# Layer 0 of a four-layer network: gate and up products split into rounded parts, ternary buffers doubled, memory laid out anew

## The chip, the cores and the metric

The kernel runs on one core of one Trainium2 chip. The metric is the device time in microseconds; the median of three runs of the kernel before is given below. A core has a matrix engine (TensorE), three engines for element-wise work (VectorE, ScalarE, GpSimd), an engine that starts transfers (SyncE), an on-chip memory of 128 partitions (SBUF) and eight banks for matrix results (PSUM). The engines run their own queues in order and wait for each other by semaphores.

## The reference, cut to what matters

The network has four layers. Each takes a layer norm of x and adds an attention branch and a feed-forward branch of it to x. The change lies in layer 0. Its attention is a linear attention with 16 heads of 16 features in chunks; its feed-forward branch has weights that a cubic spline gives from control points. Its text isn't in full here; what is computed is this:

```
xn = layernorm(x)                                   # 1024 tokens, 256 features
q, k, v = heads(xn @ wq.T), heads(xn @ wk.T), heads(xn @ wv.T)
q = (q @ fq1.T + b) * (q @ fq2.T + b) * 16 ** -0.5  # k the same with fk1, fk2
o = q @ (running sum of k.T @ v of earlier chunks) + causal(q @ k.T) @ v
o = o * rsqrt(mean(o * o) + eps) * norm_w
gate = spline_reconstruct(gate_cp, 1024, 256)       # up too; down is 256 x 1024
h = silu(xn @ gate.T) * (xn @ up.T)
x = x + o @ wo.T + h @ down.T
```

Layer 3 has weights in bf16 that are made ternary: with s the mean absolute value of a group of 64, each weight becomes -s, 0 or s, as w + (w_hat - w). This depends on the weights alone, and the kernel does it during layer 0.

## The kernel before, in words

x is held as 8 tiles of 128 tokens by 256 features, its transpose xT as two tiles (k = 0, 1) of 128 features by 1024 tokens, in two blocks (b) of 512. All float32 products of layer 0 are plain float32 matmuls; the profile shows two records for each.

**Ahead of the loop.** TensorE transposes the norm of block 0, multiplies by wq and wk (`wide`, four products to raw0), makes the first spline block (`spline`, a product with all first cubics and one with all second cubics, each for gate, up and down), does the same for block 1, then the values in four products (`tall`, g_v0) with spline blocks 2 and 3 between. ScalarE copies xT (L1147), raw0 (L1172), the first cubics (`first_cubics`, L1154) and the values (`keep_v0`, L1165) out of PSUM, and casts the six parts of the ternary weights to bf16 (`cast_ternary`, L1160). VectorE puts the second cubics over the first where a mask says so (`second_cubics`, L1530) and sums the groups of the cast parts. The splines of gate, up and down then lie in V[0], V[1] and V[2]: 2048 columns each, in four blocks (s) of 512. Then `features` makes q and k in eight steps: TensorE gives two products of a step, ScalarE copies the one to f2s (L1190, L1192; two buffers), VectorE multiplies it with the other (L1567) and multiplies k by parity (L1559).

**The loop over eight chunks** c of 128 tokens. For each, TensorE runs in this order, written out by hand: scores of 16 heads to four banks (`scores0`, L661); gate and up of block 0 for the 128 hidden rows c (`gate_up0(c, 0, 0)` and `(c, 0, 1)`); keys by values (L699); gate of block 1; the queries by the running sum (L707) and the masked scores by the values (`values0`, L679); up of block 1. The eight banks are given in turn, ten to a chunk, so that the gate of block 1 gets the bank of the chunk's first score tile, and up of block 1 that of the second. VectorE runs: four causal masks (L1596); silu times up of block 0 (`hidden0`, L1590); the mask of keys by values (L1603) and the running sum (L1606); `hidden0` of block 1; and in the first six chunks two comparisons that give the signs of one ternary part (L1611, L1612). ScalarE does the silus (L1211) and keeps the outputs.

GpSimd copies the values of chunk c+2 by parity (`by_parity`, L2063) and turns the signs into a ternary part in four operations (L2071 to L2074), in the one pair of buffers tern_t; VectorE's signs of chunk c wait for the ternary part c-1.

After the loop come the group sums (L714), the down product and the output product. Layer 1 follows; its q and k products (`split_product`, L586 to L588) already use three products of rounded parts: hi*hi, hi*lo and lo*hi, with float32r operands.

In the page of the profile "arena" and "zone" are the two halves of the working memory.

Of the kernel before, what the change touches and what calls it, by code (L numbers as in the profile page):

```python
# [9 lines left out]
F32 = mybir.dt.float32  # L10
F32R = mybir.dt.float32r
# [7 lines left out]
P = 128  # L19
# [49 lines left out]
EPS3 = 2.0 ** -23  # L69
ARENA0 = 39400  # L70
ARENA, ZONE = 22500, 17930
ARENA1 = 28120
ALL = slice(None)

# [18 lines left out]
def build(nc, dram, out):  # L93

    ctx = ExitStack()
    with ctx:  # L96
# [3 lines left out]
        def sem(name):  # L100
            return ctx.enter_context(nc.semaphore(name))
# [17 lines left out]
        bw = lB[:, B_LW:B_LW + KD * D].rearrange("p (o i) -> p o i", o=KD)  # L119
        with nc.sbuf_tensor("arena0", [P, ARENA0], F32) as arena0:  # L120
            pass
        with nc.sbuf_tensor("arena1", [P, ARENA1], F32) as arena1:
# [56 lines left out]
        def step(ins, done):  # L179
# [38 lines left out]
            sem("hsq_ready"), sem("hsq_used"), sem("ms3_ready"), sem("std3_ready"), sem("rst_loaded"))  # L218
        held, x_rest, lA_rest = sem("held"), sem("x_rest"), sem("lA_rest")
        osq_summed = sem("osq_summed")  # L220
        qk_full, v_full, wv_hi, wv_split = sem("qk_full"), sem("v_full"), sem("wv_hi"), sem("wv_split")
# [21 lines left out]

        m = Carve(arena0)
        lA = m.cols(A_END + A_END % 2)
        hid0_at = m.at
        win, phase = m.cols(SPB), m.cols(SPB)
        hid0 = Carve(arena0, hid0_at).grid(NI, T)
        m.at = hid0_at + NI * T
        f2s_at = m.at  # L250
        basis = m.cols(2 * P)
# [3 lines left out]
        silu0 = Carve(arena0, f2s_at).grid(2, BW)  # L255
        V = [m.cols(SPB) for _ in range(3)]
        raw0_at = m.at
        raw0 = m.grid(4, T)
        oT0 = Carve(arena0, raw0_at).grid(NT, D)
        q0 = m.grid(KD, T)  # L260
        k0_at = m.at
# [4 lines left out]
        kpar = [m.grid(KD, T) for _ in range(2)]  # L266
        ktok, v0 = m.grid(NT, D), m.grid(NT, D)
        xn0_at = m.at
        kvbd = m.grid(NT, D)
        xn0 = Carve(arena0, xn0_at).grid(NT, D)  # L270
        kvtmp = m.cols(D)
        vflat = [m.cols(2 * VP) for _ in range(2)]
        vpar = [v[:, 0:2 * D].rearrange("p (r w) -> p r w", r=2) for v in vflat]
        tern_t = [m.cols(512).bitcast(BF16) for _ in range(2)]

# [264 lines left out]
        def _(pe):  # L540
# [125 lines left out]
            def gate_up0(c, b, n):  # L666
                wide(g_gu0[c][b][n], lambda k: V[n][:, k * I0 + c * P:k * I0 + (c + 1) * P], xT, b)

# [46 lines left out]
            pe.wait_ge(*g_gu0[NT - 1][NB - 1][1].ready)  # L715
            for p in range(NT // 2):
                tall(g_down0[p], p, lambda t: [(hid0[:, q, tok(t)], V[2][:, q * D:(q + 1) * D]) for q in range(NI)])
# [420 lines left out]
        def _(act):  # L1138
# [18 lines left out]
            def cast_ternary(n):  # L1157
                if n == 0:
                    act.wait_ge(raw_loaded, 16)
                act.activation(w16[:, n * I0:(n + 1) * I0], raw3[:, n * I0:(n + 1) * I0], ACT.Copy).then_inc(w16_cast, 1)  # L1160

            def keep_v0(p):
                g = g_v0[p]
                act.wait_ge(*g.full)
                act.activation(v0[:, 2 * p:2 * p + 2, :], g.ps.rearrange("p (t d) -> p t d", t=2), ACT.Copy).then_inc(g.ready_sem, 1)  # L1165

            for b in range(NB):
                keep_xT(0, [b])
                for mm in range(4):
# [311 lines left out]
        def _(dve):  # L1481
# [91 lines left out]

            dve.wait_ge(*g_ktok[-1].ready)
            dve.memset(kvbd[:, 0, :], 0.0).then_inc(kvbd_ready, 1)

# [15 lines left out]
            for c in range(NT):  # L1592
# [15 lines left out]
                if c < 6:  # L1608
                    if c:
                        dve.wait_ge(tern_ready, c)  # L1610
                    dve.tensor_tensor(by_group(tern_t[0]), tern_part(c), tern_group(2, c), ALU.is_gt)  # L1611
                    dve.tensor_tensor(by_group(tern_t[1]), tern_part(c), tern_group(3, c), ALU.is_lt).then_inc(tern_signs, 1)  # L1612
# [428 lines left out]
        def _(pool):  # L2041
# [16 lines left out]
            def by_parity(c):  # L2058
# [4 lines left out]
                pool.tensor_copy(own, v0[:, c, :].rearrange("p (g r e) -> p r g e", r=2, e=DK0)).then_inc(vpar_ready, 1)  # L2063

            by_parity(0)
            by_parity(1)
            for n in range(6):
                by_parity(n + 2)
                w, (t0, t1) = tern_part(n), [by_group(t) for t in tern_t]
                pool.wait_ge(tern_signs, n + 1)  # L2070
# [5 lines left out]


            def rest(pair, whole):
                return pool.tensor_tensor(pair[1].bitcast(F32R), whole, pair[0], ALU.subtract)  # L2079

# [217 lines left out]
```

## Time and profile before

| | |
|---|---|
| median of 3 runs | 724.84 us (724.24 to 725.26) |
| the profiled execution's own time | 729.03 us |
| its span, first to last instruction | 727.4 us |
| TensorE busy | 664.4 us, 91% of the span |
| VectorE busy | 521.8 us, 72% |
| ScalarE busy | 347.3 us, 48% |
| GpSimd busy | 320.5 us, 44% |
| mean granted TensorE clock | 0.98 |

PE is TensorE, DVE is VectorE, ACT is ScalarE and POOL is GpSimd. A profile is of one execution. Times in its views count from the span's start. "Idle before" is the time in which an engine had nothing to do ahead of an instruction, with what ended it. Records of consecutive matmuls overlap, so the distance from one start to the next tells what one costs, not its length.

### The profile page before, as it was taken

The page shows a single profiled execution, that of the slowest core. Times are in us where ns is not written, and L with a number is a line of the kernel's source. Part 1 is how long each engine was busy: PE and PEld are TensorE (multiplying, and loading weights), DVE is VectorE, ACT ScalarE, POOL GpSimd, SP SyncE. Part 2 cuts the span into 40 slices and gives each one's busy share as a digit, 9 for nine tenths or more (in the row PEclk, how much of TensorE's full clock was granted, in tenths as well). Part 3 has the DMA queues.
Part 4 walks back from the last instruction along what each step waited for, and adds up shares of the span by engine and source line. Part 5 has one row for each costly group of instructions (what it writes and reads, how often), then busy time and mean ns, then how long its engine had stood idle before and what let it go on. Part 6 is the DMA issues. An engine that isn't in the chain of part 4 may idle for free. (4 is left out here: it accounts for less than half of the span.)

```text
span 727.4 us, 13380 instructions
## 1 busy us (share of the span) xinstructions
PE 664.4 (91%) x4792; PEld 495.3 (68%) x4792; DVE 521.8 (72%) x1068; ACT 347.3 (48%) x749; POOL 320.5 (44%) x255
## 2 busy tenths in 40 slices
PE   3999999999799999999999999979988699877997
PEld 2445555588477988878787978869777447545666
DVE  4287686493599799797979986565366864579794
ACT  1575111300555565756555555744454542397732
POOL 1000988300457576674747478795185301300100
PEclk9999999999999999999999999999998889999999
DMA  8701000000601010010101011114212000100001
GB/s 261 300 2 59 1 2 1 1 1 0 223 17 38 23 34 24 7 36 20 34 18 36 22 38 34 35 32 142 66 52 66 1 0 1 36 1 0 2 1 58
DMA packets 14645, 31.34 MB, mean 43 GB/s; under 512 B 1837, under 2 KB 8587, under 8 KB 14029
## 3 DMA queue, kind: packets, MB, share of 16 engines
q1 hardware_dynamic: 12813, 26.46, 11.1%
q0 software_dynamic: 1536, 3.15, 1.5%
q10 hardware_dynamic: 256, 1.18, 0.6%
q8 instruction: 27, 0.44, 0.3%
q14 instruction: 13, 0.11, 0.1%
HBM read 26.59 MB, written 5.24 MB: 44 GB/s over the span
## 5 line engine op out<-in xcount | busy, mean ns | idle before, releaser
L586 PE MATMUL bank<-zone 128*128 128x256 f32 (+1 forms) x408 | 139.6, 342 | 18.2 <-DVE arena L1663 9.1
L588 PE MATMUL bank<-zone 128*128 128x256 f32 (+1 forms) x408 | 131.4, 322 | 0.0
L587 PE MATMUL bank<-zone 128*128 128x256 f32 (+1 forms) x408 | 131.2, 322 | 0.0
L2085 POOL TENSOR_TENSOR arena<-arena 128x512 f32<-128x512 f32 x64 | 82.3, 1287 | 64.1 <-ACT arena L1262 64.1
L586 PEld LDWEIGHTS bank<-zone 128*128 128x128 f32 x408 | 77.0, 189 | 39.3 <-DVE arena L1663 14.8
L2090 POOL TENSOR_TENSOR arena<-arena 128x512 f32<-128x512 f32 x64 | 83.3, 1301 | 27.7 <-DVE arena L1663 19.0
L588 PEld LDWEIGHTS bank<-zone 128*128 128x128 f32 x408 | 76.9, 188 | 6.2
L1281 ACT ACTIVATE arena<-arena 128x256 f32<-128x256 f32 (+1 forms) x128 | 62.0, 487 | 38.4 <-DVE arena L1672 32.6
L567 PE MATMUL bank<-xT,arena 128*128 128x512 f32 x160 | 78.0, 627 | 2.1 <-DMA arena<-in_lA 0.8
L587 PEld LDWEIGHTS bank<-zone 128*128 128x128 f32 x408 | 77.1, 189 | 3.5
L1672 DVE CUSTOM_DVE_ANT_0 arena<-bank,const 128x256 f32<-128x256 f32 (+1 forms) x128 | 45.6, 403 | 29.0 <-PE bank L773 22.1
L1688 DVE SCALAR_TENSOR_TENSOR x<-bank,arena,x 128x256 f32<-128x256 f32 x128 | 52.9, 470 | 13.3 <-PE bank L588 11.8
L1662 DVE TENSOR_TENSOR arena<-bank,arena 64x512 f32<-64x512 f32 x64 | 44.3, 693 | 18.2 <-ACT arena L1262 15.7
L803 PE MATMUL bank<-arena 128*128 128x128 f32 x256 | 50.8, 281 | 2.3 <-issue 2.3
L567 PEld LDWEIGHTS bank<-xT,arena 128*128 128x128 f32 x160 | 29.5, 197 | 34.1 <-issue 29.8
L1262 ACT ACTIVATE arena<-bank 128x512 f32<-128x512 f32 x64 | 37.5, 587 | 30.1 <-PE bank L588 30.1
L2079 POOL TENSOR_TENSOR zone<-arena,zone 128x512 fp32r<-128x512 f32 (+1 forms) x42 | 44.6, 1070 | 15.2 <-DMA arena<-in_cossin 6.1
L2048 POOL TENSOR_TENSOR lnw<-lnw,minus_half 128x4 f32<-128x4 f32 x8 | 8.2, 1020 | 97.6 <-DVE lnw L1500 97.6
L1023 PE MATMUL bank<-zone 128*128 128x512 f32 x128 | 36.8, 417 | 11.4 <-DVE arena L1918 9.2
L802 PE MATMUL bank<-arena 128*128 128x128 f32 x224 | 45.9, 288 | 0.0
L1663 DVE TENSOR_TENSOR arena<-bank,arena 64x512 f32<-64x512 f32 x64 | 43.7, 683 | 0.8
L803 PEld LDWEIGHTS bank<-arena 128*128 128x128 f32 x256 | 41.2, 197 | 3.9 <-issue 2.6
(289 smaller groups left out, 1345.9 us busy)
## 6 DMA issues: line engine op xcount, KB each, us to landing
arena<-in_qk SPq DMA_DIRECT2D x16, 256.0 KB
arena<-in_tern SPq DMA_DIRECT2D x1, 3072.0 KB, 22.6
arena<-in_wv SPq DMA_DIRECT2D x8, 256.0 KB, 2.9
arena<-in_wo SPq DMA_DIRECT2D x16, 128.0 KB, 2.1
arena<-in_wr SPq DMA_DIRECT2D x1, 1792.0 KB, 11.5
lB<-in_lB SPq DMA_DIRECT2D x1, 1288.5 KB, 25.1
x<-in_x SPq DMA_DIRECT2D x2, 512.0 KB, 8.0
xg_rows<-arena SPq DMA_DIRECT2D x1, 1024.0 KB
```

The source lines that it names most:

```text
L567: last = pe.matmul(g.ps, weight(k), act[:, k, b * BW:(b + 1) * BW], start=(k == 0), stop=(k == KD - 1))
L586: pe.matmul(dst, lhi, rhi, start=(n == 0), stop=False)
L587: pe.matmul(dst, lhi, rlo, start=False, stop=False)
L588: last = pe.matmul(dst, llo, rhi, start=False, stop=(n == len(terms) - 1 and not open_end))
L802: pe.matmul(ps[6 + g // 2][:, tok(t % TPB)], v1[:, t - 1, mine], pT1[:, t, 0, :], start=True, stop=False)
L803: last = pe.matmul(ps[6 + g // 2][:, tok(t % TPB)], v1[:, t, mine], pT1[:, t, 1, :], start=(t == 0), stop=True)
L1281: last = act.activation(S1[:, t, lo:], S1[:, t, lo:], ACT.Exp, scale=-1.0, bias=nmax[:, t:t + 1], accum_out=rsum[:, t:t + 1])
L1672: last = dve.tensor_tensor_reduce(S1[:, t, lo:], ps[2 + g % 2][:, tt * 2 * P + lo:(tt + 1) * 2 * P], winmask[:, lo:], -SC1, 3.0e38, ALU.ad ...
L1688: last = dve.scalar_tensor_tensor(out=x[:, t, :], in0=ps[bank][:, tt * D:(tt + 1) * D], scalar=rinv[:, t:t + 1], in1=x[:, t, :], op0=ALU.m ...
L2079: return pool.tensor_tensor(pair[1].bitcast(F32R), whole, pair[0], ALU.subtract)
L2085: pool.tensor_tensor(qraw[:, j, :], qraw[:, j, :], cosT[:, at], ALU.mult).then_inc(cos_done, 1)
L2090: pool.tensor_tensor((kT1, qT1)[j % 2][:, at], qraw[:, j, :], qsin[:, j, :], ALU.add).then_inc(qk_ready, 1)
```

## The change

- gate_up0 no longer multiplies V by xT in float32. xT and the splines of gate and up are each split into a rounded part (float32r) and the remainder, and each product becomes `split_product`: six matmuls of 512 columns.
- ScalarE makes the rounded parts: of xT in `round_x0(b)` (two operations a block, after the first cubics of the block), of the splines in `round_gu0(s)` (two a spline block, placed as the diff shows, s = 3 after the third of the eight feature steps). round_gu0 waits until all four remainders of xT are made.
- GpSimd makes the remainders: `rest_of_x0`, `rest_of_gu0`, one operation for each of ScalarE's.
- The parts of the spline weights (gu0p) lie where hid0, the hidden tiles, go: the remainder part of chunk c in the second half of its own hidden tile, the rounded part in the first half of the next chunk's tile.
- The two buffers of tern_t become two pairs; the signs of chunk c wait for ternary part c-2.
- The running sum kvbd lies over V[1], tern_t over V[0]; so VectorE waits for all remainders (gu0_split 8) before it clears kvbd, and for all ternary parts after the loop.
- basis, smask, V and lA and what follows are at other columns; a tensor "early" takes the first 7424 columns - 1280 of basis and mask and 6144 of V.

```diff
-ARENA0 = 39400
+ARENA0 = 40430
+EARLY = 2 * P + 3 * SPB + SPB // 2
...
+        kvbd = Carve(arena0, V_at + SPB).grid(NT, D)
...
+        x0p = [Carve(zone, at).grid(KD, T) for at in (m.at - ARENA, m.at - ARENA + KD * T)]
...
+        gu0p = [by_chunk(hid0_at - ARENA + T), by_chunk(hid0_at - ARENA + BW)]
+
+        def spline_block(n, s):
+            at = V_at + n * SPB + s * BW
+            return early[:, at:at + BW].rearrange("p (c i) -> p c i", c=TPB)
+
+        def split_block(part, n, s):
+            at = n * D + s // 2 * P
+            return gu0p[part][:, s % 2 * TPB:s % 2 * TPB + TPB, at:at + P]
...
             def gate_up0(c, b, n):
-                wide(g_gu0[c][b][n], lambda k: V[n][:, k * I0 + c * P:k * I0 + (c + 1) * P], xT, b)
+                g = g_gu0[c][b][n]
+                reuse(g)
+                split_product(g.ps, [(cut(parts(gu0p), ALL, c, slice(n * D + k * P, n * D + (k + 1) * P)),
+                                      cut(parts(x0p), ALL, k, slice(b * BW, (b + 1) * BW))) for k in range(KD)]).then_inc(g.full_sem, 1)
...
                 if c == 0:
-                    pe.wait_ge(*g_spl[-1][-1][1].ready)
+                    pe.wait_ge(x0_split, NB * KD)
+                if c % TPB == 0:
+                    pe.wait_ge(gu0_split, 6 + c // TPB * 2)
...
+            def round_x0(b):
+                act.wait_ge(xT_ready, KD * (b + 1))
+                for k in range(KD):
+                    act.activation(x0p[0][:, k, b * BW:(b + 1) * BW].bitcast(F32R), xT[:, k, b * BW:(b + 1) * BW], ACT.Copy).then_inc(x0_hi, 1)
+
+            def round_gu0(s):
+                act.wait_ge(x0_split, NB * KD)
+                for n in range(2):
+                    act.wait_ge(*g_spl[s][n][1].ready)
+                    act.activation(split_block(0, n, s).bitcast(F32R), spline_block(n, s), ACT.Copy).then_inc(gu0_hi, 1)
...
                 first_cubics(b)
+                round_x0(b)
             for b in range(NB):
                 keep_v0(2 * b)
+                if b == 0:
+                    round_gu0(0)
                 cast_ternary(2 + 2 * b)
                 keep_v0(2 * b + 1)
                 cast_ternary(3 + 2 * b)
                 first_cubics(NB + b)
+                round_gu0(1 + b)
...
+                if n == 2:
+                    round_gu0(3)
...
+            dve.wait_ge(gu0_split, 8)
             dve.memset(kvbd[:, 0, :], 0.0).then_inc(kvbd_ready, 1)
...
-                    if c:
-                        dve.wait_ge(tern_ready, c)
+                    if c >= 2:
+                        dve.wait_ge(tern_ready, c - 1)
...
+            dve.wait_ge(tern_ready, 6)
...
+            for b in range(NB):
+                rest_of_x0(b)
+            pool.wait_ge(x0_split, NB * KD)
+            rest_of_gu0(0)
             by_parity(0)
             by_parity(1)
+            for s in range(1, 4):
+                rest_of_gu0(s)
```

## Rows read from the trace of the kernel before

**Rows 1.** Busy time and instructions of each engine, granted clock and transfers, the loop.

```profile
60.00:145.00 85.00, 84.47 (x680) 45.73 (x675) 55.52 (x86) 20.25 (x39) 54.95 (x30) 1.00 0.04 14
```

**Rows 2.** Order of time, TensorE: start, length, instruction; loop's start, one chunk, loop's end.

```profile
59.03 1.17 PE L661 MATMUL bank<-arena 32*128 32x128 f32 x32 [0.89 <-DVE arena L1559]
...
79.13 1.17 PE L661 MATMUL bank<-arena 32*128 32x128 f32 x32
80.23 3.70 PE L567 MATMUL bank<-xT,arena 128*128 128x512 f32 x8
83.77 0.61 PE L699 MATMUL bank<-arena 128*128 128x128 f32 x4
84.22 1.88 PE L567 MATMUL bank<-xT,arena 128*128 128x512 f32 x4
85.94 0.61 PE L707 MATMUL bank<-arena 128*128 128x128 f32 x4
...
87.49 1.98 PE L567 MATMUL bank<-xT,arena 128*128 128x512 f32 x4
89.40 1.17 PE L661 MATMUL bank<-arena 32*128 32x128 f32 x32
...
141.56 3.60 PE L714 MATMUL bank<-arena,const 128*128 128x512 f32 x8
```

**Rows 3.** Order of time, VectorE, in the same chunk and the next.

```profile
80.15 1.23 DVE L1611 TENSOR_TENSOR arena<-w,tern_s 128x1024 bf16<-128x1024 bf16 x1 [0.22 <-POOL w L2074]
81.29 1.42 DVE L1612 TENSOR_TENSOR arena<-w,tern_s 128x1024 bf16<-128x1024 bf16 x1
82.64 2.47 DVE L1596 TENSOR_TENSOR arena<-bank,const 128x512 f32<-128x512 f32 x4
...
86.07 1.11 DVE L1606 TENSOR_TENSOR arena<-arena 128x256 f32<-128x256 f32 x1
89.51 0.69 DVE L1590 TENSOR_TENSOR arena<-bank,arena 128x512 f32<-128x512 f32 x1 [2.33 <-PE bank L567]
90.94 1.23 DVE L1611 TENSOR_TENSOR arena<-w,tern_s 128x1024 bf16<-128x1024 bf16 x1 [0.73 <-POOL w L2074]
```

**Rows 4.** Order of time, GpSimd, in the same chunk.

```profile
80.18 1.46 POOL L2063 COPY arena<-arena 128x256 f32<-128x256 f32 x1
82.80 2.13 POOL L2071 TENSOR_TENSOR arena<-arena 128x1024 bf16<-128x1024 bf16 x1 [1.16 <-DVE arena L1612]
85.00 1.89 POOL L2072 TENSOR_TENSOR arena<-arena,tern_s 128x1024 bf16<-128x1024 bf16 x1
```

**Rows 5.** Order of time, TensorE: first and last of layer 1's first twelve split matmuls.

```profile
193.07 0.47 PE L586 MATMUL bank<-zone 128*128 128x512 f32 x1 [1.62 <-POOL zone L2079]
...
195.71 0.40 PE L588 MATMUL bank<-zone 128*128 128x512 f32 x1
```

**Rows 6.** Order of time, GpSimd and VectorE, in layer 2.

```profile
577.92 4.51 POOL L2165 TENSOR_TENSOR x<-x,bias 128x2048 f32<-128x2048 f32 x1 [1.50 <-DVE arena L1503]
...
578.48 3.98 DVE L1857 TENSOR_SCALAR arena<-arena 128x2 f32<-128x2 f32 x1
```

**Rows 7.** Order of time, TensorE, ahead of the loop.

```profile
27.08 7.13 PE L567 MATMUL bank<-xT,arena 128*128 128x512 f32 x16 [0.75 <-ACT xT L1147]
```

**Rows 8.** Groups by line and form: busy, mean ns of one, idle before; rounding and remainder.

```profile
L1428 ACT ACTIVATE zone<-arena 128x512 fp32r<-128x512 f32 x16 | 9.9, 616 | 0.0
...
L2079 POOL TENSOR_TENSOR zone<-arena,zone 128x512 fp32r<-128x512 f32 x25 | 32.0, 1292 | 11.5 <-DMA arena<-in_cossin 6.1 <-ACT zone L1346 5.4
```

**Rows 9.** Busy time of ScalarE alone, first cubics of block 1 to the features.

```profile
35.69:50.17 14.48, 10.66 (x18) 1.00 0.01 2
```

**Rows 10.** Busy time of TensorE, then the granted clock, in three stretches.

```profile
475.00:478.00 3.00, 1.22 (x11) 1.00 0.00 0
550.00:553.00 3.00, 0.71 (x13) 0.81 0.44 109
553.00:556.00 3.00, 3.00 (x15) 0.50 0.08 27
```

More of the change, by code:

```diff
@@ L120, in build @@
         with nc.sbuf_tensor("arena0", [P, ARENA0], F32) as arena0:
+            pass
+        with nc.sbuf_tensor("early", [P, EARLY], F32) as early:
             pass
@@ L219, in build @@
         held, x_rest, lA_rest = sem("held"), sem("x_rest"), sem("lA_rest")
+        x0_hi, x0_split, gu0_hi, gu0_split = sem("x0_hi"), sem("x0_split"), sem("gu0_hi"), sem("gu0_split")
         osq_summed = sem("osq_summed")
@@ L241, in build @@
         y_rows = nc.dram_tensor("y_rows", (SLOTS + 1, D), F32, kind="Internal").ap()
[L244 to L249, printed above, removed]
+        m = Carve(early)
         f2s_at = m.at
-        basis = m.cols(2 * P)
+        basis = Carve(arena0, m.at).cols(2 * P)
+        m.at += 2 * P
         smask4 = m.cols(SPB // 2).bitcast(I32)
@@ L255, in build @@
         silu0 = Carve(arena0, f2s_at).grid(2, BW)
+        kvtmp = Carve(arena0, f2s_at + 2 * BW).cols(D)
+        V_at = m.at
         V = [m.cols(SPB) for _ in range(3)]
+        tern_t = Carve(arena0, V_at).cols(SPB).bitcast(BF16).rearrange("p (s n e) -> p s n e", s=2, n=2)
+        kvbd = Carve(arena0, V_at + SPB).grid(NT, D)
+        assert m.at == EARLY
+        m = Carve(arena0, m.at)
+        lA = m.cols(A_END + -A_END % 16)
         raw0_at = m.at
@@ L259, in build @@
         oT0 = Carve(arena0, raw0_at).grid(NT, D)
+        win, phase = [Carve(arena0, m.at + n * SPB).cols(SPB) for n in range(2)]
         q0 = m.grid(KD, T)
@@ L266, in build, with by_chunk @@
         kpar = [m.grid(KD, T) for _ in range(2)]
[L267 to L271, printed above, removed]
+        ktok = m.grid(NT, D)
+        hid0_at = m.at
+        assert hid0_at >= ARENA
+        hid0 = m.grid(NI, T)
+        m.cols(BW)
+        x0p = [Carve(zone, at).grid(KD, T) for at in (m.at - ARENA, m.at - ARENA + KD * T)]
+        m.cols(2 * KD * T + 128)
         vflat = [m.cols(2 * VP) for _ in range(2)]
         vpar = [v[:, 0:2 * D].rearrange("p (r w) -> p r w", r=2) for v in vflat]
-        tern_t = [m.cols(512).bitcast(BF16) for _ in range(2)]
+        xn0 = Carve(arena0, m.at).grid(NT, D)
+        v0 = m.grid(NT, D)
+        def by_chunk(at):
+            return zone[:, at:at + NI * T].rearrange("p (c w) -> p c w", c=NI)[:, :, 0:BW]
+        gu0p = [by_chunk(hid0_at - ARENA + T), by_chunk(hid0_at - ARENA + BW)]
[5 more added lines that the diff above has]
+            return gu0p[part][:, s % 2 * TPB:s % 2 * TPB + TPB, at:at + P]
         def by_group(t):
@@ L715, in _ @@
             pe.wait_ge(*g_gu0[NT - 1][NB - 1][1].ready)
+            pe.wait_ge(*g_spl[-1][-1][1].ready)
             for p in range(NT // 2):
@@ L1608, in _ @@
                 if c < 6:
-                    if c:
-                        dve.wait_ge(tern_ready, c)
-                    dve.tensor_tensor(by_group(tern_t[0]), tern_part(c), tern_group(2, c), ALU.is_gt)
-                    dve.tensor_tensor(by_group(tern_t[1]), tern_part(c), tern_group(3, c), ALU.is_lt).then_inc(tern_signs, 1)
+                    if c >= 2:
+                        dve.wait_ge(tern_ready, c - 1)
+                    dve.tensor_tensor(by_group(tern_t[:, c % 2, 0, :]), tern_part(c), tern_group(2, c), ALU.is_gt)
+                    dve.tensor_tensor(by_group(tern_t[:, c % 2, 1, :]), tern_part(c), tern_group(3, c), ALU.is_lt).then_inc(tern_signs, 1)
             dve.wait_ge(ln3_ready, 1)
+            dve.wait_ge(tern_ready, 6)
             after(k2)
@@ L2063, in by_parity, with rest, rest_of_x0, rest_of_gu0 @@
                 pool.tensor_copy(own, v0[:, c, :].rearrange("p (g r e) -> p r g e", r=2, e=DK0)).then_inc(vpar_ready, 1)
+            def rest(pair, whole):
+                return pool.tensor_tensor(pair[1].bitcast(F32R), whole, pair[0], ALU.subtract)
+            def rest_of_x0(b):
+                for k in range(KD):
+                    pool.wait_ge(x0_hi, KD * b + k + 1)
+                    rest([t[:, k, b * BW:(b + 1) * BW] for t in x0p], xT[:, k, b * BW:(b + 1) * BW]).then_inc(x0_split, 1)
+            def rest_of_gu0(s):
+                for n in range(2):
+                    pool.wait_ge(gu0_hi, 2 * s + n + 1)
+                    rest([split_block(part, n, s) for part in range(2)], spline_block(n, s)).then_inc(gu0_split, 1)
+            for b in range(NB):
+                rest_of_x0(b)
+            pool.wait_ge(x0_split, NB * KD)
+            rest_of_gu0(0)
             by_parity(0)
             by_parity(1)
+            for s in range(1, 4):
+                rest_of_gu0(s)
             for n in range(6):
                 by_parity(n + 2)
-                w, (t0, t1) = tern_part(n), [by_group(t) for t in tern_t]
+                w, (t0, t1) = tern_part(n), [by_group(tern_t[:, n % 2, i, :]) for i in range(2)]
                 pool.wait_ge(tern_signs, n + 1)
@@ L2075, in _ @@
                 pool.wait_ge(tern_ready, n + 1)
-            def rest(pair, whole):
-                return pool.tensor_tensor(pair[1].bitcast(F32R), whole, pair[0], ALU.subtract)
             def turn_qk(h, js, base=HEAD0):
```

## The prediction, made before the changed kernel was run

> **What bounds the kernel now.** I read the busy shares of the stretch of layer 0's eight chunks first, then TensorE's order of time in one chunk, then VectorE's and GpSimd's in the same chunk. TensorE is busy for 84.47 of 85 us there at full clock [rows 1], so a cheaper product is worth something only as long as no other engine takes its place. The loop runs from the scores at 59.03 to the group sums at 141.56, 82.5 us [rows 2]. A full chunk is 10.27 us (79.13 to 89.40): scores 1.10, two feed-forward products 3.54, keys by values 0.44, third product 1.72, read of the running sum and values 1.55, fourth product 1.91. Beside it runs the ternary ring: VectorE's two sign operations start at 80.15 and again at 90.94 [rows 3], 10.79 apart; in between lie the signs (to 82.71) and GpSimd's four operations on the only buffer pair (82.80 to 90.9) [rows 4]. It is the longer of the two and takes over within a few chunks, once its lead is used up: eight chunks at TensorE's pace would be 81.3.
>
> **Part 1, the products.** A plain product is two float32 matmuls, 1.71 to 1.91 us here. A split one is six single-pass matmuls. The row that shows them back to back is layer 1's: twelve from 193.07 to the start of the last at 195.71 [rows 5], so 0.23 each with 0.11 once for the change of kind. A pair of products then takes 2.87 (3.54 before), a single one 1.49 (1.72 and 1.91 before). TensorE's own chunk falls from 10.27 to 8.98 (0.67, 0.23 and 0.42 less). If nothing else held it: chunk 0 8.4 (no read of the sum), chunks 1 to 6 9.0, chunk 7 8.5: 70.9, a gain of 11.6 us. That is the upper end for this part.
>
> **Part 2, the doubled ternary buffers.** The ring through one buffer pair is broken: the signs of chunk c now wait for ternary c-2. But VectorE and GpSimd come to work at the same time on operands in SBUF, and the trace shows what that costs. A VectorE operation on 2 elements takes 3.98 us, started at 578.48 while GpSimd's addition on x ran from 577.92 to 582.43 [rows 6]: it waits for the whole of the other's instruction. The running sum (L1606) at 86.07 ends 0.29 after GpSimd's operation that started at 85.00 [rows 3, 4]. The other way, GpSimd's copy issued at 80.18 ends at 81.64, 0.35 after the first sign operation gives way at 81.29, and the second sign operation is lengthened to 1.42: GpSimd gets in between the two. Operations with one input in PSUM (the four masks, 2.47 in all at 82.64 [rows 3] with GpSimd busy) don't suffer.
>
> Before, the ring itself kept signs and ternary work apart; that cover is gone. GpSimd needs 8.1 us for a ternary part and 0.4 for the copy (0.35 of it behind the sign operation), so in a chunk of 9 to 10 us one of its operations nearly always runs when the signs are issued. Signs then: rest of the running operation about 0.8 (0 to 1.9), first sign 1.1, a whole GpSimd operation 1.8 (it waited, so it goes next) in most cases, second sign 1.1: 4.4, against 2.28 alone (80.15 to 81.29, twice); bounds 2.3 and 5.9. What is queued behind them on VectorE is the four masks of the next chunk, and TensorE waits for the first mask to free the bank of its third product. Counted from the end of a fourth product: hidden 0.7, signs 4.4, first mask 0.65, then third product 1.49, sum and values 1.55, fourth product 1.49: 10.3 to 10.4, more than TensorE's 8.98. The signs of chunk 0 meet an idle GpSimd, those of chunk 1 and 2 are at 3.8 to 4.1 (GpSimd has not yet filled its time), so the chunks are 8.4, 9.0, 9.8, 10.1, 10.4, 10.4, 10.4, 8.5: 77.1. The same count for the code before gives 82.4 against 82.5 read. **Loop: 5.4 us less**, between 11.6 less (no meeting) and 2.4 more (signs at 5.9 make the five chunks 11.8, 84.9 in all).
>
> The exclusive use is also a rule of the Trainium skill (SBUF — State Buffer, Who interferes with whom): a VectorE instruction with two SBUF inputs and a GpSimd instruction that reads SBUF shut each other out for the whole instruction. The trace agrees: 3.98 us for two elements. It speaks against doubling, whose overlap it takes back.
>
> The waits moved with it cost nothing: ternary 5 is done some 6 us before VectorE leaves the loop, and GpSimd's copies for chunk n+2 stand one ternary part behind, over 10 us before TensorE needs them.
>
> **Part 3, the rounding ahead of the loop.** ScalarE gets four rounded pieces of x and eight blocks of weights, each 128x512 from SBUF. Such a rounding is 0.62 long and a remainder on GpSimd, of which there are twelve, 1.29 [rows 8]. Back to back I count a rounding at 0.52: an estimate from the masks and the running sum, whose records overlap the next start by about 0.1. VectorE and ScalarE set this stretch, since the features need the last spline block.
> - The two roundings of x's first half stand in ScalarE's queue ahead of the copies of the second xT, for which TensorE already waits 0.75 at 27.08 [rows 7]: 1.05 late.
> - From the first cubics of block 1 to the features (14.48 us) ScalarE works 10.66 [rows 9]: 3.8 idle, of which the last 1.8 is the wait for VectorE's block 3. Into it go, ahead of the last cubics, six roundings (3.15) and a wait for GpSimd's last remainder of x (two remainders 2.6, less the copy that ScalarE does meanwhile and their overlap: 1.8). 4.95, of which 2.0 fit in the idle pieces: 2.9 late. The two of block 2 fit into the last 1.8.
> - The two of block 3 (1.05) stand in the features, where ScalarE and VectorE take turns: 0.9.
> Sum **4.8 us more**. Below: 3.0, if the wait for x's remainders is shorter and more of it falls in idle time; above: 6.1, if VectorE's predicated copies (mask in SBUF; the trace has none beside a GpSimd read) hold up one remainder, 1.29, on the way to ScalarE's first weights; 7 with a second. The last remainder of the weights ends near 60; VectorE's new wait for it stands behind all its feature products and parities, and TensorE's scores, which need most of these, start at 59.03 + 4.8: it is covered by some 4 us; without that it would cost up to the remainder's 1.29.
>
> **Part 4, the layout** only names other columns; the DMAs, their order and sizes stay: 0, within the 0.5 us to either side by which the runs shown differ.
>
> **The sum.** -5.4 + 4.8 = -0.6 us. The profiled execution took 729.03 with a span of 727.4 and would take 728.4; the median of the runs is 4.2 lower, 724.84, and becomes 724.2. Nothing behind the loop changes, and it is bound by TensorE again at once.
>
> **Rivals.**
> - A. The forecast: exclusive use eats half the product gain, the prologue the rest. 724.2, own range 722 to 727. Chance 0.42.
> - B. The meeting is milder: the sign pair stays together (GpSimd gets in only before or after), signs 2.6 to 3.3. Chunks near 9.1, with two of 9.7: loop 72.4, -10; or none at all, -11.6. With +4.8: 718.0 to 719.6. For it: in the ring before, only a short copy shows the order. Against it: 1.42 instead of 1.23 for the second sign in every chunk. 0.20.
> - C. Slower: TensorE's clock falls among the features. There it will wait about 1.7 us for the last first cubics and 1.2 for VectorE's part of block 3, with one feature group of some 0.8 us before, between and after. In the trace the granted clock was 0.81 of full speed in a stretch in which TensorE worked only 0.71 of 3 us, and 0.50, the 1.2 GHz level, in the next; it was 1.00, 2.4 GHz, in another with 1.22 of 3 [rows 10]. At 1.2 GHz the six feature groups after that take 1.64 instead of 0.82 and pass the 0.8 of ScalarE and VectorE: +2 to +3.2 over A, 726.2 to 727.4, say 727. It decides if the clock falls ahead of the fourth group. For it: the gaps; against: they come one by one, with groups between. 0.25.
> - D. The prologue costs 3 or less with A's loop: 722.4 or less. ScalarE's order is written out, so little speaks for more. 0.13.
>
> By the Trainium skill (TensorE: Matmul & The Clock Gate, the warm start-to-start rule of N / 2.4 + 2.5 ns) a 512-column matmul would follow each 216 ns; rows 5 show 230 to 240. By the rule TensorE's chunk would be 8.6, an estimate, and only chunks 0, 1 and 7 would show it, 1 us in all; the row decides.
>
> **How the numbers follow.** About 0.2% (1.45 us) can be told from no change. A splits into 0.12 faster, 0.24 same, 0.06 slower; B is faster; C 0.05 same, 0.20 slower; D 0.10 faster, 0.03 same: 0.42, 0.32, 0.26. The range takes in B's upper part and C with a dearer prologue: 718.6 to 728.6; the likeliest one's own is 722 to 727.
>
> **What the profile after would show.** The third product in a full chunk at 1.5; scores 8.4 and 9.0 apart in the first two chunks and 10 to 10.5 in chunks 3 to 6; the sign operations at 1.2 to 3 us each with GpSimd running through, and TensorE's third product waiting for the masks. Scores of chunk 0 near 63.8 instead of 59.03; a ScalarE gap of 1.8 in front of the first weight rounding, and features 4 us later. It is wrong if signs stay at 1.2 each (B), if the clock row of the features is below 1.00 (C), or if the scores start before 62 (D).

## The result, and the profile after

The changed kernel takes 727.65 us (median of 6 runs, 726.99 to 727.96), the kernel before 725.05 beside it (6 runs, 724.24 to 725.71): ratio 1.0033, 95% interval 1.0021 to 1.0044. It is slower, by 0.3%. The forecast was 724.2, inside a range of 718.6 to 728.6. The profiled execution took 727.57 us, with a span of 726.0.

TensorE's order of time in the trace of the changed kernel: start, length, instruction, and in brackets the idle time before. Split products are L611 to L613, scores L686, keys by values L729, the sum's read L737, values L707, group sums L744.

```profile
28.15 7.13 PE L592 MATMUL bank<-xT,arena 128*128 128x512 f32 x16 [1.77 <-ACT xT L1178]
...
64.03 1.17 PE L686 MATMUL bank<-arena 32*128 32x128 f32 x32 [0.65 <-DVE arena L1607]
...
85.50 0.61 PE L729 MATMUL bank<-arena 128*128 128x128 f32 x4
87.38 0.50 PE L611 MATMUL bank<-zone 128*128 128x512 f32 x1 [1.27 <-DVE arena L1645]
...
88.87 0.61 PE L737 MATMUL bank<-arena 128*128 128x128 f32 x4
89.41 1.08 PE L707 MATMUL bank<-arena 128*32 128x128 f32 x32
90.42 0.49 PE L611 MATMUL bank<-zone 128*128 128x512 f32 x1
...
92.01 1.17 PE L686 MATMUL bank<-arena 32*128 32x128 f32 x32
...
108.82 0.49 PE L611 MATMUL bank<-zone 128*128 128x512 f32 x1 [1.55 <-DVE arena L1645]
...
143.47 3.59 PE L744 MATMUL bank<-arena,const 128*128 128x512 f32 x8
```

Against [rows 2], the third product now takes 1.49 (87.38 to 88.87) where it took 1.72, and the values follow. But ahead of it stands a wait for VectorE's mask (L1645) that the chunk of [rows 2] did not have. The scores of the first chunk start at 64.03 instead of 59.03, the group sums at 143.47 instead of 141.56: a loop of 79.4 us instead of 82.5. The idle time at 28.15 is 1.77 where [rows 7] have 0.75.

VectorE and GpSimd in chunk 4 of the changed kernel (signs L1660 and L1661; ternary operations L2140 to L2143; copy by parity L2113), first VectorE, then GpSimd:

```profile
103.36 1.71 DVE L1660 TENSOR_TENSOR arena<-w,tern_s 128x1024 bf16<-128x1024 bf16 x1
105.00 3.16 DVE L1661 TENSOR_TENSOR arena<-w,tern_s 128x1024 bf16<-128x1024 bf16 x1
108.08 2.47 DVE L1645 TENSOR_TENSOR arena<-bank,const 128x512 f32<-128x512 f32 x4
```

```profile
97.59 2.15 POOL L2140 TENSOR_TENSOR arena<-arena 128x1024 bf16<-128x1024 bf16 x1
99.82 1.90 POOL L2141 TENSOR_TENSOR arena<-arena,tern_s 128x1024 bf16<-128x1024 bf16 x1
101.80 2.19 POOL L2142 TENSOR_TENSOR arena<-arena,w 128x1024 bf16<-128x1024 bf16 x1
104.07 3.01 POOL L2143 TENSOR_TENSOR w<-w,arena 128x1024 bf16<-128x1024 bf16 x1
107.14 1.27 POOL L2113 COPY arena<-arena 128x256 f32<-128x256 f32 x1
108.38 2.14 POOL L2140 TENSOR_TENSOR arena<-arena 128x1024 bf16<-128x1024 bf16 x1
```

The reader is to see three things. The two engines alternate: the first sign is issued at 103.36 and gets its turn as the third operation ends (101.80 + 2.19 = 103.99), GpSimd's fourth operation is issued at 104.07 and is lengthened to 3.01, and the second sign takes 3.16 because it waits for the end of that fourth operation at 107.08 (104.07 + 3.01). GpSimd has no idle time in brackets any more: its cycle, 97.59 to 108.38, is 10.79 us, and that is what a chunk lasts, as long as VectorE's sign cycle was before (80.15 to 90.94 [rows 3]). And the third operation takes 2.19 us. I had carried over 8.1 us for the four from [rows 4]; the rows of before for the third and fourth, which had no contention at all, are these:

```profile
97.77 1.95 POOL L2073 TENSOR_TENSOR arena<-arena,w 128x1024 bf16<-128x1024 bf16 x1
99.80 1.89 POOL L2074 TENSOR_TENSOR w<-w,arena 128x1024 bf16<-128x1024 bf16 x1
```

The same operation of the same shape on the same data has become 0.24 us longer without anything beside it; the experiments below find out why.

### The profile page after: what moved, and what is told of

The parts are those of the page before. It is cut to its first block and busy times, and to the rows that moved or that the text cites. A ratio compares the mean times of both kernels' runs of the same rounds, so it can differ in the third digit from the quotient of the medians.

```text
span 726.0 us, 13538 instructions
## 1 busy us (share of the span) xinstructions
PE 653.4 (90%) x4856; PEld 506.2 (70%) x4856; DVE 533.8 (74%) x1068; ACT 353.0 (49%) x761; POOL 340.7 (47%) x267
## 5 line engine op out<-in xcount | busy, mean ns | idle before, releaser
L611 PE MATMUL bank<-zone 128*128 128x256 f32 (+1 forms) x472 | 167.6, 355 | 22.4 <-DVE arena L1645 7.4
L613 PE MATMUL bank<-zone 128*128 128x256 f32 (+1 forms) x472 | 157.0, 333 | 0.0
L612 PE MATMUL bank<-zone 128*128 128x256 f32 (+1 forms) x472 | 156.9, 332 | 0.0
L611 PEld LDWEIGHTS bank<-zone 128*128 128x128 f32 x472 | 89.2, 189 | 49.0 <-DVE arena L1713 12.8
L613 PEld LDWEIGHTS bank<-zone 128*128 128x128 f32 x472 | 89.2, 189 | 9.1
L612 PEld LDWEIGHTS bank<-zone 128*128 128x128 f32 x472 | 89.4, 189 | 5.3
L1310 ACT ACTIVATE arena<-bank 128x512 f32<-128x512 f32 x64 | 37.6, 587 | 31.0 <-PE bank L613 30.9
L834 PE MATMUL bank<-arena 128*128 128x128 f32 x256 | 49.5, 275 | 2.3 <-issue 2.3
L833 PE MATMUL bank<-arena 128*128 128x128 f32 x224 | 44.9, 282 | 0.1
L2244 POOL TENSOR_TENSOR arena<-arena,minus_half 128x4 f32<-128x4 f32 x2 | 2.9, 1468 | 86.2 <-DVE arena L1982 86.2
L1291 ACT ACTIVATE arena<-bank 128x512 f32<-128x512 f32 x32 | 19.1, 598 | 47.6 <-PE bank L613 47.6
```

The lines of the kernel that those rows point to most:

```text
L611: pe.matmul(dst, lhi, rhi, start=(n == 0), stop=False)
L612: pe.matmul(dst, lhi, rlo, start=False, stop=False)
L613: last = pe.matmul(dst, llo, rhi, start=False, stop=(n == len(terms) - 1 and not open_end))
L833: pe.matmul(ps[6 + g // 2][:, tok(t % TPB)], v1[:, t - 1, mine], pT1[:, t, 0, :], start=True, stop=False)
L834: last = pe.matmul(ps[6 + g // 2][:, tok(t % TPB)], v1[:, t, mine], pT1[:, t, 1, :], start=(t == 0), stop=True)
```

## The experiments

All are compared with the kernel before, measured beside them. "Scores" is the time from TensorE's transposes of block 1 (25.28 in the changed kernel) to the first scores; "loop" is from there to the group sums. From the group sums to the issue of the transfer of layer 1's first weights all have 41.5 to 41.8 us. What lies behind that differs from one profile to the next: 539.6 to 543.1 us, but 534.8 to 536.8 in the four of e8 to e11, and 544.3 in the profile shown ahead of the prediction. So the profiled waypoints tell the terms apart, and the ratios check the sum. In the kernel before: scores 33.8, loop 82.5, GpSimd's third and fourth operation 1.96 and 1.89.

**e0, the kernel before again.**

> The kernel before, unchanged, for a second profile. Theory: the profiled execution shown before the prediction (729.0 us against a median of 724.8) was held up behind the loop, by a late transfer at 184 to 192 us and lower granted clock at 545 to 560 us; another one takes 725 to 726 us, with the loop again from 59.0 to 141.6 us. Rival: recording itself costs 4 us, and it is 729 again.

723.53 us, scores 33.8, loop 82.5. The waypoints repeat to 0.02. The span is 5.5 us shorter than that of the profile shown ahead of the prediction: 1.0 of it lies ahead of the transposes, 4.5 behind the loop.

**e1, the doubled buffers alone.** Edit, to the kernel before:

```diff
-        tern_t = [m.cols(512).bitcast(BF16) for _ in range(2)]
+        tern_t = m.cols(2 * I0).bitcast(BF16).rearrange("p (s n e) -> p s n e", s=2, n=2)
...
-                    if c:
-                        dve.wait_ge(tern_ready, c)
+                    if c >= 2:
+                        dve.wait_ge(tern_ready, c - 1)
```

> The kernel before with the doubled ternary buffers alone. Theory (port): VectorE's signs and GpSimd's operations exclude each other, so GpSimd's cycle stays 10.8 us (8.1 of its own, 0.4 copy, 2.3 of signs) with or without the second pair; loop 82 to 83 us, total 724.5 to 725.5 us. Rival (ring): the wait for the one pair was what held the chunks at 10.8, without it they run at TensorE's 10.27; loop 81.2 us, total 723.7 us or less.

723.9 us, 0.9992 (0.9975 to 1.0009); loop 81.6, third and fourth operation 1.96 and 1.89, GpSimd's cycle 10.61 instead of 10.79. The loop lies between the two expectations, 82 to 83 and 81.2, since most of its chunks run at TensorE's 10.27 here and only the seventh reaches 10.61. What tells is the cycle: doubling alone frees 0.2 us a chunk. The ring through one buffer pair was broken, and the alternation keeps nearly all of its length.

**e2, the changed kernel with one buffer pair.** Edit: `tern_t[:, 0, ...]` and `wait_ge(tern_ready, c)` in place of `c % 2` and `c - 1`.

> The changed kernel with one ternary pair and the old wait. Port: the cycle of 10.8 us is the same, only one early chunk can lose; 727.6 to 728.8 us. Ring: the loop falls back to the 82.5 us of the kernel before; 730.5 us or more.

729.41 us, 1.0072 (1.005 to 1.0094); scores 38.7, loop 81.8, the cycle 11.3 (two chunks in the middle, 12.85 and 9.71, have that as their mean). So doubling is worth 2.3 us in the loop beside the split products, and it did not cause the loss. One pair with these products should have given at most the 10.8 of before. It gave 11.3, and its third and fourth operations take 2.19 and 2.14.

**e3, all the rounding, but plain products.** Leaves out the products with remainder parts:

```diff
-                split_product(g.ps, [...]).then_inc(g.full_sem, 1)
+                wide(g, lambda k: gu0p[0][:, c, n * D + k * P:n * D + (k + 1) * P], x0p[0], b)
```

> The changed kernel with all roundings and remainders made, but gate and up as plain float32 products of the rounded parts, so that the remainders are not used (the output leaves out the two cross products). Theory: the start of the loop stays at 64.0 us, 5.0 later than before, and the loop is 82 to 83 us again: 729.5 to 731 us. The split products are then worth the 3 us between this and the changed kernel. Rival: the rounding is cheap and the loss lies in the loop; then this is at 725 to 727 us.

732.63 us, 1.0123 (1.0093 to 1.0152); scores 38.7, loop 83.9. Beside e1, with the same products and the same doubled pairs, the loop is 2.3 us longer, and GpSimd's cycle 11.07 instead of 10.61: 0.46 a chunk, which is what the third and fourth operation (2.18 and 2.12) have more. What differs between the two in the loop is where things lie.

**e4, without GpSimd's four ternary operations** (left out, with the values that they make):

> The changed kernel without GpSimd's four ternary operations (they are left out, so layer 3's weights are not ternary); VectorE's signs stay. Port: nothing shuts the signs out, they take 1.1 us each, every full chunk is 9.0 us, the loop 70.9 us instead of 79.4, total 719 us. Rival: VectorE or the order of the chunk sets 10 us or more whatever GpSimd does; loop 78 us or more, 726 us or more.

719.26 us, 0.9927 (0.9905 to 0.9949); the loop is 70.7, the chunks 8.97 each. Part 1 of the prediction said 70.9 and 8.98, so all that is missing from the product's gain is GpSimd's work. Scores came 40.4 after the transposes, later than in any kernel so far, and the stretch windows show why (columns: busy time of TensorE, its weight loads, VectorE, ScalarE and GpSimd, then granted clock, DMA share and GB/s):

```profile
24.00:27.00 3.00, 1.23 (x9) 0.99 (x10) 1.96 (x3) 2.68 (x6) 1.67 (x2) 0.95 0.90 382
27.00:30.00 3.00, 3.00 (x4) 1.25 (x5) 0.00 (x0) 0.00 (x0) 0.82 (x1) 0.50 0.96 400
30.00:33.00 3.00, 3.00 (x8) 1.33 (x7) 0.00 (x0) 1.20 (x2) 0.00 (x0) 0.99 0.41 159
```

TensorE has the same 1.77 us of idle time as in the changed kernel's first row, all of it in the first window, and then runs at 0.50 of the clock, the 1.2 GHz level, for 3 us. It costs 40.4 - 38.7 = 1.7 us. In the profile of the changed kernel the same gap passed at 1.00, for 27 to 30 us and 30 to 33:

```profile
27.00:30.00 3.00, 1.85 (x5) 0.90 (x6) 0.38 (x1) 1.09 (x3) 2.24 (x2) 1.00 1.00 417
30.00:33.00 3.00, 3.00 (x9) 1.33 (x8) 0.00 (x0) 1.19 (x2) 0.00 (x0) 1.00 0.47 183
```

The 1.23 there and the 1.85 here don't tell the two apart: the windows cut the same gap at different places. In the 3 us that end 0.15 us ahead of the product behind the gap, TensorE is busy for 1.38 in e4 and 1.37 in the changed kernel, and in the 3 us after them the clock is 0.52 in the one and 1.00 in the other. Of the eleven profiles with a gap of 1.77 us (the changed kernel, e2 to e6, e9, e12 to e15) the clock fell in three, e4, e5 and e14; it fell in none of those with 0.75. What decides it isn't shown.

**e5, the signs one chunk later and ahead of the masks.**

```diff
+                if 0 < c < 7:
+                    signs(c - 1)
```

> The changed kernel with the signs of chunk c moved behind the running sum of chunk c+1, so that the next chunk's masks no longer stand behind them. Port: the signs still take some 4.7 us, but TensorE's third product no longer waits for them; chunks of 9.2 to 10.3 us as GpSimd's lag is taken up by the second pair, loop 74 to 77 us, total 723 to 725.5 us. Rival: GpSimd's cycle of 10.8 us binds through the wait for the part before last, and nothing is won: 727 to 728 us.

724.99 us, 1.0004 (0.9986 to 1.0022); loop 76.3: the first five chunks run at 8.5 to 8.97 and the last three at 10.6 to 10.8. The signs no longer stand ahead of the masks, so TensorE keeps its own pace until GpSimd, never idle from chunk 3 on, sets the cycle: 10.79 again, though both signs now take 3.2 us and stand elsewhere. GpSimd's first part starts 16.5 us after the first scores instead of 11.7, and its last ends 3.1 us behind the group sums. The clock fell at 27 us (0.66 and 0.77 in the two windows), which took 1.7 of the gain back.

**e6, no wait of ScalarE's weight rounding for x's remainders.** Edit: the line `act.wait_ge(x0_split, NB * KD)` taken out.

> The changed kernel without ScalarE's wait for all remainders of xT ahead of the first weight rounding (the parts lie in different places). ScalarE's idle 1.6 us at 39.8 to 41.5 us goes: scores at 62.3 instead of 64.0 us, total 725.9 us. Rival: VectorE or TensorE is late anyway there, and the total stays at 727.6 us.

725.08 us, 1.0007 (0.9993 to 1.0022); scores 37.0 instead of 38.7, loop 79.4. The wait, 1.61 us in this row of ScalarE of the changed kernel, costs 1.7:

```profile
41.46 1.15 ACT L1202 ACTIVATE zone<-early 128x512 fp32r<-128x512 f32 x2 [1.61 <-POOL zone L2116]
```

**e7, the roundings in ScalarE's idle slots** of the second block, with the wait gone:

```diff
+                    if b and mm == 0:
+                        round_x0(0)
+                    elif b and mm < 3:
+                        round_gu0(0, [mm - 1])
...
-                round_x0(b)
+                if b:
+                    round_x0(1)
...
-            for b in range(NB):
-                rest_of_x0(b)
-            pool.wait_ge(x0_split, NB * KD)
+            rest_of_x0(0)
             rest_of_gu0(0)
+            rest_of_x0(1)
```

> As the one without the wait, and the roundings of xT block 0 and of the first spline block moved to where ScalarE waits for the products of block 1 (28 to 35 us). TensorE no longer waits 1.8 us at 28 us, and only four roundings and the two among the features are left on the way: scores at 60.5 to 61.5 us, total 724.2 to 725.2 us. Rival: ScalarE's place in the order was not what cost it (remainders on GpSimd or VectorE's copies were), and the scores stay above 62.3 us.

723.95 us, 0.9988 (0.9975 to 1.0002); scores 35.4, loop 79.4. 3.4 of the 4.95 us ahead of the loop are a matter of order and waits, not of work. The roundings of x now lie behind the second xT, and TensorE's gap at 27 us is 0.75 again.

**e8, e5 and e7 together.**

> Early slots and later signs in one kernel. If the loss ahead of the loop and the port contention in it are independent terms, they add up: the scores start as in e7 (+35.4 us after the second block's first transposes, against +38.7 in the changed kernel), since the signs lie behind the loop's start; the loop lasts as in e5 (76.3 us against 79.4), so the total is 3.4 + 3.2 = 6.6 us under the changed kernel, about 721 us. Rival: the one hides the other (the later signs need time that the longer loop gave them, or TensorE's granted clock falls behind its gap at 27 us as in e5, which costs 1.7 us): then 722.5 to 724 us.

715.34 us beside 719.73 of the kernel before: 0.9935 (0.9921 to 0.9949). Scores 35.4, loop 76.3, clock 1.00 at 27 us: the terms add. The kernel before took 719.73 beside all of e8 to e11, some 5 us less than beside the others. The profiles have this difference behind the loop, where part of it is the granted clock: 0.93 in e8 against 0.86 in e5 and e6, for 50 us from 400 us behind the group sums. The loops don't have it, so only ratios are compared across the two.

**e9, two columns.** The changed kernel with V, and so the buffers over it, 8 bytes further:

```diff
-EARLY = 2 * P + 3 * SPB + SPB // 2
+EARLY = 2 * P + 3 * SPB + SPB // 2 + 16
...
+        m.at += 2
         V_at = m.at
         V = [m.cols(SPB) for _ in range(3)]
+        m.at += 14
```

> The changed kernel with the GpSimd ternary buffer (and V, kvbd) two fp32 columns further, nothing else. Theory (alignment): GpSimd's third and fourth ternary operation took 2.19 and 2.12 us in the changed kernel, where the buffer begins on a multiple of 16 bytes, and 1.96 and 1.89 us before, where it began 8 bytes off; 8 bytes off again they take 1.96 and 1.89, GpSimd's cycle is 10.3 us instead of 10.8, the loop 77.1 us instead of 79.4, the total 725.3 us. Rival (place): it is where in the partition the buffer and the weights lie, or how VectorE's operations fall beside them; two columns change nothing, 2.19 and 2.12 stay, the loop stays 79.4 us, the total 727.6 us.

719.67 us beside 719.73: 0.9998 (0.9979 to 1.0016); loop 76.9. GpSimd's third and fourth operation and VectorE's two signs and masks, at the start of the chunk of e9 that begins at 100.4, first GpSimd, then VectorE:

```profile
99.56 1.95 POOL L2144 TENSOR_TENSOR arena<-arena,w 128x1024 bf16<-128x1024 bf16 x1
101.59 2.75 POOL L2145 TENSOR_TENSOR w<-w,arena 128x1024 bf16<-128x1024 bf16 x1
```

```profile
101.13 1.47 DVE L1662 TENSOR_TENSOR arena<-w,tern_s 128x1024 bf16<-128x1024 bf16 x1
102.52 2.91 DVE L1663 TENSOR_TENSOR arena<-w,tern_s 128x1024 bf16<-128x1024 bf16 x1
105.35 2.47 DVE L1647 TENSOR_TENSOR arena<-bank,const 128x512 f32<-128x512 f32 x4
```

The third is back at 1.95, the fourth, with its wait for the sign, at 2.75 instead of 3.01, and the cycle at 10.29. Scores are 38.4.

**e11, the kernel before with only its buffer pair moved**, from 8 bytes off a multiple of 16 onto one (`m.at += 2` ahead of tern_t).

> The kernel before with the ternary buffer moved by two fp32 columns, from 8 bytes off a multiple of 16 onto one; nothing else. Theory (alignment): GpSimd's third and fourth operation go from 1.96 and 1.89 us to 2.19 and 2.12, its cycle in the loop from 10.8 to 11.25 us, the loop from 82.5 to about 84.5 us, the total from 724.9 to about 727 us. Rival (place): nothing changes, loop 82.5 us, total 724.9 us.

721.89 beside 719.73: 1.0026 (1.0009 to 1.0043); scores 33.8, loop 84.8, 2.3 more. The old kernel shows the loss without any other part of the change:

```profile
98.72 2.18 POOL L2074 TENSOR_TENSOR arena<-arena,w 128x1024 bf16<-128x1024 bf16 x1
100.98 2.12 POOL L2075 TENSOR_TENSOR w<-w,arena 128x1024 bf16<-128x1024 bf16 x1
```

**e12 to e15: by itself, or against the other input?** Third and fourth operation read the buffer pair and the bf16 weights. e12 is the changed kernel again; e13 moves the weights alone by 8 bytes, e14 both by 8, e15 the pair alone by one column, 4 bytes. Edits of e13 and e14 (e14 with e9's as well), and of e15 (with e9's `EARLY`, and 15 columns behind V):

```diff
-        w16 = sb("w16", TERN, BF16)[:, :]
+        w16 = sb("w16", TERN + 16, BF16)[:, 4:4 + TERN]
```

```diff
+        m.at += 1
         V_at = m.at
...
+        m.at += 15
```

> The changed kernel as it is, beside its variants. Third and fourth ternary operation 2.19 and 2.12 us without a meeting, loop 79.4 us, 0.33% over the kernel before (0.2 to 0.45%).

> The changed kernel with the bf16 ternary weights 8 bytes further (off a multiple of 16), the buffer pair where it was (on one). Theory relative: what costs is that the two inputs of the operation begin at the same place within 16 bytes; now they differ by 8 as in the kernel before: third and fourth operation 1.96 and 1.89 us, cycle 10.3, loop 76.9 us, 2.5 us less than the changed kernel. Theory absolute: what costs is that the buffer pair begins on a multiple of 16 bytes: 2.19 and 2.12 stay, loop 79.4 us.

> The changed kernel with both the buffer pair and the weights 8 bytes off a multiple of 16. Theory relative: the inputs begin at the same place again: 2.19 and 2.12 us, loop 79.4 us, as the changed kernel. Theory absolute: the buffer pair is off a multiple of 16: 1.96 and 1.89 us, loop 76.9 us.

> As the run with two columns, but one (4 bytes). If only the same place within 16 bytes costs: 1.96 and 1.89 us, loop 76.9 us. If it counts by 8 bytes (two words lie in the same half of 16): 2.19 and 2.12 us or something between, loop 78 to 79.4 us.

| | pair, bytes off 16 | weights | third, mean ns | loop, us | ratio (interval) |
|---|---|---|---|---|---|
| e12 | 0 | 0 | 2198 | 79.4 | 1.0040 (1.0024 to 1.0055) |
| e13 | 0 | 8 | 1955 | 76.9 | 1.0003 (0.9989 to 1.0018) |
| e14 | 8 | 8 | 2200 | 79.4 | 1.0033 (1.0019 to 1.0047) |
| e15 | 4 | 0 | 2007 | 77.1 | 1.0000 (0.9988 to 1.0013) |

The groups by line, GpSimd's third operation, of e12, e13, e14 and e15:

```profile
L2142 POOL TENSOR_TENSOR arena<-arena,w 128x1024 bf16<-128x1024 bf16 x6 | 13.2, 2198 | 0.5
```

```profile
L2142 POOL TENSOR_TENSOR arena<-arena,w 128x1024 bf16<-128x1024 bf16 x6 | 11.7, 1955 | 0.5
```

```profile
L2144 POOL TENSOR_TENSOR arena<-arena,w 128x1024 bf16<-128x1024 bf16 x6 | 13.2, 2200 | 0.5
```

```profile
L2144 POOL TENSOR_TENSOR arena<-arena,w 128x1024 bf16<-128x1024 bf16 x6 | 12.0, 2007 | 0.5
```

Scores are 38.7 in e12, e13 and e15; in e14 they are 40.1, and its clock was 0.50 from 27 to 30 us, as in e4.

Theory relative holds and theory absolute falls, twice: moving the weights cures it though the pair stays on a multiple of 16, and moving the pair off it brings nothing once the weights move along. GpSimd is slower in this operation when its two inputs begin at the same place within 16 bytes; 4 bytes apart do nearly as well as 8, which neither expectation of e15 had. The runs moved the starts by 4 or 8 bytes only, so they don't tell whether it repeats every 16 bytes or at a larger step; nor do they show the reason.

**e10, the version that the findings point to.** e7's slots, later signs, e9's columns, signs of parts 0 to 3 in chunks 1 to 4 and of parts 4 and 5 behind the loop, where the wait for all parts now stands ahead of the down product's sums:

```diff
+                if 0 < c < 5:
+                    signs(c - 1)
...
+            signs(4)
+            signs(5)
             for p, g in enumerate(g_sum0):
...
-                by_parity(n + 2)
+                if n < 5:
+                    by_parity(n + 2)
+                if n == 4:
+                    by_parity(7)
```

> Early slots, later signs, the two columns of e9, and the six ternary parts spread: GpSimd copies the chunks' halves first where a chunk waits for them, parts 0 to 3 lie in chunks 1 to 4, the signs of parts 4 and 5 behind the loop. Theory (GpSimd's cycle of copy, two signs and four operations sets the chunk, and only chunks with signs pay): signs in four chunks instead of six; the loop is 71 to 73 us (e4, without any ternary work on GpSimd, had 70.7), the scores start +35.4 us as in e7, nothing is late behind the loop, total 715 to 718 us. Rival: the parts left over make the first block of layer 1 or the weights behind them late, so that what the loop gains is given back there: loop 72 but the total 720 to 724 us.

709.67 us beside 719.73: 0.9855 (0.9839 to 0.9871), faster than both kernels. Scores 35.0, loop 71.5 of e4's 70.7, and the group sums to layer 1 still 41.6. TensorE's busy time in its loop, columns as above:

```profile
59.81:131.27 71.46, 71.14 (x761) 56.80 (x761) 54.58 (x79) 17.91 (x36) 36.48 (x22) 1.00 0.05 16
```

It is busy for 71.14 of 71.46 us; in the changed kernel it is 72.06 of 79.5:

```profile
64.00:143.50 79.50, 72.06 (x761) 57.11 (x762) 66.22 (x83) 17.92 (x37) 60.44 (x30) 1.00 0.04 15
```

GpSimd's work of four parts fills the loop and that of the last two lies behind it, where its next operation starts at 134.82, and nobody waits for it.

## Why the prediction was wrong

**The step that failed is Part 4: "names other columns ...: 0".** The prediction put at nothing what turned out to be worth 2.3 to 2.5 us: the loop is 79.4 with the inputs in step and 76.9 with them 8 bytes apart (e12, e13), and 2.3 is what the move alone adds to the kernel before (e11). In time measured on one chip that is 727.38 - 725.34 = 2.0, the 0.4% of e12 against the 0.0% of e13. With it the sum -0.6 becomes about +1.8; 2.6 was measured, with an interval of 1.5 to 3.2, which holds 1.8. The 0.8 between is not told apart by any run. Part of it can be the clock at the gap at 27 us: three of eleven profiles with 1.7 us each are some 0.5 on the mean, an estimate. I had looked at what the layout does to transfers and never asked what an address does to the speed of an operation, so no bound stood for it in the range. That 0.23 us on each of two operations counts nearly in full is due to GpSimd's cycle, which sets the later chunks in both kernels: the move costs 2.3 in the kernel before as well (e11).

**Part 1 was right:** TensorE's own chunk of 8.98 is 8.97 in e4, its loop of 70.9 is 70.7; third product 1.49. That it fits to 0.01 is luck: 10.27 less the 0.67, 0.23 and 0.42 given is 8.95. The lower figure of 8.6 is not what came.

**Part 2 was right in its mechanism, and with the columns put right also in size.** Signs of 4.4 us are 4.3 in e9 (101.13 to 105.43), the chunks of 10.4 are 10.3, the loop of 77.1 is 76.9. The 4.4 itself fits better than its parts: 0.8, 1.1, 1.8 and 1.1 add up to 4.8, and the whole operation, counted as coming in most cases, comes in every chunk of the steady cycle; it is the rest of the running operation that was smaller, 0.3 in e9. In the changed kernel the signs take 4.8 (103.36 to 108.16) and the chunks 10.8. What I read less well is who sets it. I counted VectorE's queue up to TensorE's third product, and both counts come out nearly alike; but GpSimd is never idle, and the chunk is its sum: from start to start 2.23, 1.98, 2.27, 3.07 and 1.24, 10.79. e5 speaks for GpSimd: with the signs moved away from ahead of the masks, the cycle was 10.79 again once GpSimd was never idle. Seen so, the doubling could not bring much from the outset, 0.2 us a chunk alone (e1) and 0.5 beside the split products (e2): two signs and four operations exclude each other with one buffer pair or with two. The Trainium skill (SBUF — State Buffer, Who interferes with whom) says the two instructions shut each other out for the whole instruction; the trace agrees, with 3.16 us for a sign of 1.23, whose two inputs both lie in SBUF. The runs also show what e10 uses: parts made outside the full chunks cost nothing there. Masks with an input in PSUM are free of it: 2.47 for four with GpSimd busy, 2.48 with it idle.

**Part 3 was right:** 4.95 us for 4.8. The 1.05 at the second xT is 1.02 (1.77 against 0.75); the wait of ScalarE, forecast at 1.8, is 1.61 long and costs 1.7 (e6). The other items were not measured one by one.

**Rivals.** B, a milder meeting, fell: the pair of signs did not stay together. C named a cost that exists, at the wrong place. The clock of the changed kernel's profile stayed at 1.00 among the features; where it fell, in e4, e5 and e14, it was after the gap at 27 us that Part 3's own first item had made. It did not fall in the profile of the changed kernel, so it does not explain that execution (727.57, beside a median of 727.65), but in one where it does it costs 1.7 us more; which of the timed runs had it stays open. D fell: 4.95 us, not 3. That the measured time lies in the range is luck: the range reached as far up as it did because of C, and the cause was not in it.

## What to carry to other kernels

- Before doubling a buffer between two engines, ask whether the buffer keeps them apart or a shared resource does. If their instructions exclude each other anyway, add up both engines' instructions: here the sum was nearly the cycle, with one pair or two (10.79 and 10.61 in e0 and e1). What shortened the loop was to move work to a stretch without contention (e10, with e7's and e9's edits: 0.9855).
- A relayout is a change of speed until shown otherwise. Compare the mean of each operation of the loop between two kernels, uncontended ones first: 1.96 against 2.19 stood in plain sight in the first trace after.
- Work added to a queue ahead of a stage is paid by its place: 3.4 of 4.95 us were gone once the roundings stood in gaps that the queue had and a wait was gone (e7).

## What the runs showed of the hardware

- A GpSimd operation on two bf16 inputs of 128x1024 took 1.95 to 1.96 us with the inputs beginning 8 bytes apart within 16, 2.01 with 4, and 2.19 to 2.20 with both at the same place (e12 to e15), for the third; the fourth took 1.89 at 8 bytes apart and 2.12 at the same place (before and e11). The first operation, whose two inputs lie in the same place in all these kernels, takes 2.13 to 2.17 in those without a meeting, which fits; moving one of its inputs was not tried.
- The two engines took turns throughout the loops: of VectorE and GpSimd, whichever was waiting went next when the other's instruction ended. A GpSimd operation of 2.12 issued 1.0 us ahead of the end of a sign (104.07 and 105.07) showed 3.01, 0.89 more.
- After the same gap of 1.77 us in TensorE's work the clock fell to 0.50 for 3 us in one execution (e4) and stayed at 1.00 in another (the changed kernel).
